# A graph layer's edge stage rebuilt: keys compared as products of sign codes, and a scatter with split sources and fp32 weights

## The reference, cut to what matters

```python
bias = jnp.full((n, n), NEG); bias = bias.at[diag, diag].set(0.0)
bias = bias.at[dst, src].set(edge_weight)      # of equal (dst, src) the last edge stays
scores = einsum('hnd,hmd->hnm', q, k) / 8 + bias[None]        # layer 0, 8 heads
sums = segment_sum(beta[dst], src)                            # layer 1: how often each edge occurs
adj = zeros((N, N)).at[edge_index[0], edge_index[1]].set(1.0) # layer 2: whether it occurs
```

## Time and profile before

| | us |
|---|---|
| median of 3 runs | 592.97 (591.87 to 593.33) |
| the profiled execution's own time | 593.2 |
| its span | 591.3 |
| PE busy | 482.4 |
| DVE busy | 357.6 |
| ACT busy | 205.7 |
| POOL busy | 149.2 |

### The profile page before, as it was taken

The page is one execution under the profiler, slowest core; times in us unless marked ns, Lnnn a source line. Parts: engine busy times, 40 slices in busy tenths (PEclk is TensorE's granted clock), DMA queues, the critical chain, the costliest instruction groups (busy, mean ns, idle before and its releaser), DMA issues.

```text
span 591.3 us, 9566 instructions
## 1 busy us (share of the span) xinstructions
PE 482.4 (82%) x3050; PEld 286.8 (48%) x3050; DVE 357.6 (60%) x890; ACT 205.7 (35%) x408; POOL 149.2 (25%) x153
## 2 busy tenths in 40 slices
PE   4999465677675699999799899767768679999996
PEld 2444222677665599944344444445533234444442
DVE  6699998788887996457813410369992520064305
ACT  1244233998986757322210111313332111101110
POOL 6033330333332810012100610055554110011000
PEclk9999865756766869999899999989988859999998
DMA  6994000000000300439240020000000000000001
GB/s 190 395 414 174 0 1 0 3 0 0 0 0 24 119 1 2 172 114 355 71 125 1 0 72 0 0 0 1 1 0 1 0 0 1 1 0 1 0 1 71
DMA packets 14456, 34.14 MB, mean 58 GB/s; under 512 B 992, under 2 KB 1504, under 8 KB 13920
## 3 DMA queue, kind: packets, MB, share of 16 engines
q1 hardware_dynamic: 14432, 33.83, 15.8%
HBM read 32.71 MB, written 1.11 MB: 57 GB/s over the span
## 4 chain that ended last, share of the span: by engine, by line
PE 48%; DVE 26%; issue 11%; ACT 5%; DVEq 4%; DMA 3%; POOL 2%; ACTq 1%; POOLq 0%; SPq 0%
PE ring L1002 33%; PE bank L1105 5%; PE ring L1008 4%; DVE RB L743 4%; DVE G L951 3%; DVE G L947 3%; DVE G L962 3%; DVEq L743 2%; PE ring L1201 2%; DMA G<-key_scratch 2%; DVE st L889 2%; ACT RB L552 2%; PE ring L1188 1%; DVE G L847 1%; DVE W_SD L797 1%
## 5 line engine op out<-in xcount | busy, mean ns | idle before, releaser
L1063 PE MATMUL bank<-rhs_now,X 128*128 128x64 bf16 x512 | 58.3, 210 | 23.5 <-DVE rhs_now L782 22.3
L743 DVE SCALAR_TENSOR_TENSOR RB<-G,tr,HH 128x256 bf16<-128x256 f32 (+1 forms) x128 | 64.3, 566 | 9.0 <-DMA G<-key_scratch 5.1
L1063 PEld LDWEIGHTS bank<-rhs_now,X 128*128 128x128 bf16 x512 | 50.6, 102 | 29.7 <-DVE rhs_now L782 29.4
L1064 PE MATMUL bank<-rhs_now,X 128*128 128x32 bf16 x512 | 57.3, 204 | 0.0
L1065 PE MATMUL bank<-rhs_now,X 128*128 128x32 bf16 x512 | 56.3, 185 | 0.0
L458 POOL TENSOR_TENSOR RB<-X,vec 128x512 f32<-128x512 f32 x16 | 21.9, 1379 | 125.0 <-DVE X L898 117.6
L1065 PEld LDWEIGHTS bank<-rhs_now,X 128*128 128x128 bf16 x512 | 52.7, 121 | 0.0
L1064 PEld LDWEIGHTS bank<-rhs_now,X 128*128 128x128 bf16 x512 | 51.0, 103 | 0.0
L438 POOL TENSOR_TENSOR A_SD<-A_SD,HH 128x128 f32 x64 | 30.6, 478 | 74.6 <-ACT HH L578 63.9
L909 DVE TENSOR_TENSOR HH<-ring,RB 128x512 f32<-128x512 f32 x16 | 11.0, 686 | 61.3 <-PE ring L1002 46.3
L1049 PE MATMUL ring<-KB,QB 64*128 64x512 f32 x64 | 29.5, 747 | 20.2 <-ACT G L519 20.2
(11 more groups left out here) (159 smaller groups left out, 965.2 us busy)
## 6 DMA issues: line engine op xcount, KB each, us to landing
G<-key_scratch SPq DMA_DIRECT2D x3, 2048.0 KB, 21.8
WAF<-in_wqkv SPq DMA_DIRECT2D x2, 1024.0 KB, 9.6
WB<-in_wo SPq DMA_DIRECT2D x2, 1024.0 KB, 17.0
WC<-in_w SPq DMA_DIRECT2D x2, 1024.0 KB, 17.0
WAF<-in_w SPq DMA_DIRECT2D x2, 1024.0 KB, 8.8
G<-in_w SPq DMA_DIRECT2D x1, 2048.0 KB, 14.7
G<-key_scratch SPq DMA_DIRECT2D x1, 1536.0 KB, 10.2
WAF<-in_xT SPq DMA_DIRECT2D x4, 256.0 KB, 5.4
```

The source lines that it names most:

```text
L743: dve.scalar_tensor_tensor(out=junk[:, j, 0:width], in0=G[:, bass.ds((t0 + j) * P, width)], scalar=keyT[:, bass.ds(t0 + j, 1)], in1=later_ ...
L1063: nc.tensor.matmul(gb[:, b, :, :], src1, rhs_now[:, q, j, 0:2, :], start=(j == 0), stop=False)
L1064: nc.tensor.matmul(gb[:, b, 1, :], src1, rhs_now[:, q, j, 2, :], start=False, stop=False)
```

## The change

**Keys.** The key becomes an integer of 18 bits. DVE takes each bit out (18 instructions), and one instruction makes it +16 or -16 in bf16. With three more rows (one, minus the position, the position, and constants) each tile has 24 rows of 128. SP stores these 768 KB and loads them back as `rows_l` and `rows_r`, with each code row on one partition, tiles 0 to 63 on partitions 0 to 20 and the rest from 64 on. A product of 21 rows is then above zero exactly where two keys are equal and the second position is later. TensorE makes three 128x128 products of each pair of tiles, and DVE takes the maximum of each row. Two such pairs make one step, of which there are 32, laid between the 16 products of K.

**Scatter.** The source is split into its low 7 bits, one-hot over 128 partitions, and its high 2 bits, which together with the dst in the window choose one of 128 columns. So a group is four 128x128 products: two bf16 for the counts and two fp32 for the weights. DVE makes the one-hots for four groups (eight tiles, a chunk, 16 in all) with one instruction each for sources and columns, and one for the fp32 weights; ACT widens the sources to fp32. `S` and `V` move into the scatter, two or three products ahead of each chunk.

**Clearing of the bias.** ACT writes `free` = relu(1 - count) beside the counts, and GpSimd multiplies the bias window by it, then adds the counts; DVE only adds the weights.

**Moved.** `wo0` is loaded after `bias_built`, since its tensor holds the wide sources. GpSimd adds the bias to V after its last group. `pe.wait_ge(tile_ranges, 2)`, ahead of Q, comes after the new codes on DVE.

```diff
             # SP
-            sp.dma_start(key_dram, nat[:, 3, :]).then_inc(key_stored, 16)
-                load(f"key{c}", G[:, part], flat[part].partition_broadcast(P))
+            sp.wait_ge(code_ready, 3)
+            sp.dma_start(code_dram, code).then_inc(code_stored, 16)
+            load("wk0", WA[:, 1, :, :], blocks(a["wqkv0"][:, D:2 * D]))
+            sp.wait_ge(code_stored, 16)
+            for i in range(2):
+                of_half = code_dram[i * (NT // 2):(i + 1) * (NT // 2), :, :]
+                part = slice(i * 64, i * 64 + ROWS)                      # ROWS = 21
+                sp.dma_start(by_tile(rows_l[part, :]), of_half[:, 0:ROWS, :].rearrange("t k e -> k t e")
+                             ).then_inc(loads["rows"], 16)
...                                     # rows_r: 18 rows, then 3 rows
             # GpSimd, for each group
+                held = W_SD[:, :, bass.ds(base, WIN)]
+                pool.wait_ge(free_ready, g + 1)
+                pool.wait_ge(group_folded, g + GI)
+                pool.tensor_tensor(held, held, free_g[:, q, :, :], ALU.mult).then_inc(bias_cleared, 1)
             # ACT
+            def widen(slot_, count, lap):
+                act.wait_ge(src_hot_ready, count)
+                if lap is not None:
+                    act.wait_ge(group_full, lap)
+                act.activation(src_wide[:, slot_, :, :, :], src_hot[:, slot_, :, :, :],
+                               ACT.Copy).then_inc(src_wide_ready, 1)
...
+                act.wait_ge(bias_cleared, g + 1)
+                act.activation(free_g[:, q, :, :], group_bank[q][:, 0, :, :], ACT.Relu, bias=one[:, :],
+                               scale=-1.0).then_inc(free_ready, 1)
+                act.activation(cnt_g[:, q, :, :], group_bank[q][:, 0, :, :], ACT.Copy).then_inc(count_ready, 1)
             # DVE
+            for k in range(CODE):                                       # CODE = 18
+                dve.tensor_scalar(bits_i[:, k, :], key_i, k, 1, ALU.logical_shift_right,
+                                  ALU.bitwise_and).then_inc(edges_float, 1)
...
+            dve.tensor_scalar(code[:, 3:ROWS, :], bits_i[:, :, :], 2.0 * BIT, -BIT, ALU.mult,
+                              ALU.add).then_inc(code_ready, 1)
...
+            def hot(out_, keys):
+                return dve.tensor_tensor(out_, iota_2[:, :, :].rearrange("p (q n) j -> p q n j", q=1).broadcast_to(
+                    [P, GI, P, 2]), keys.rearrange("p (q n j) -> p q n j", n=1, j=2).broadcast_to([P, GI, P, 2]),
+                    ALU.is_equal)                                       # all bf16
...
+            for p in range(PAIRS):                                      # PAIRS = 32
+                dve.wait_ge(pair_full, p + 1)
+                dve.tensor_reduce(later[:, 2 * p:2 * p + 2, :],
+                                  bank_all[:, p % 2 * 2:p % 2 * 2 + 2, 0:3 * P].rearrange("p r (c e) -> p r c e", e=P),
+                                  AX.X, ALU.max).then_inc(pair_taken, 1)
...
+                for c in range(NI):                                     # NI = 16
+                    word = dve.value_load(packed_i[0:1, c:c + 1], min_val=0, max_val=(1 << 28) - 1)
+                    g, more = c * GI, c + 2 < NI
+                    for q in range(GI):
+                        if more and q == GI - 2:
+                            dve.wait_ge(group_full, g + GI)
+                            dve.wait_ge(src_wide_ready, c + 1)
+                            src_hots(c % 2, chunk(lo_key, c + 2))
+                        if more and q == GI - 1:
+                            weight_hots(c % 2, chunk(last_weight, c + 2), c + 3)
+                        fold(g + q, q, window_start(word, q))
+                        if more and q == GI - 2:
+                            dst_hots(c % 2, chunk(column_key, c + 2))
             # TensorE
+            def compare(p):
+                if p >= 2:
+                    pe.wait_ge(pair_taken, p - 1)
+                for i in range(2):
...
+                    nc.tensor.matmul(to[:, 0:2 * P], rows_l[part, e:e + P], rows_r[part, e:e + 2 * P], start=True,
+                                     stop=True)
+                    last = nc.tensor.matmul(to[:, 2 * P:3 * P], rows_l[part, e + P:e + 2 * P],
+                                            rows_r[part, e + P:e + 2 * P], start=True, stop=True)
+                last.then_inc(pair_full, 1)
...
+                for j in range(2):
+                    nc.tensor.matmul(counts, src_hot[:, slot_, q, :, j], dst_hot[:, slot_, q, :, j], start=(j == 0),
+                                     stop=(j == 1), skip_group_check=True)
+                for j in range(2):
+                    last = nc.tensor.matmul(weights, src_wide[:, slot_, q, :, j], weight_hot[:, slot_, q, :, j],
+                                            start=False, stop=(j == 1), skip_group_check=True)
```

More of the change, by code:

```diff
@@ L34, with beside_scatter @@
 UNIT_HEADS = [0, 2, 1, 3, 4, 6, 5, 7]
+def beside_scatter():
+    return [[("S", 2 * (c // NB), c % NB), ("S", 2 * (c // NB) + 1, c % NB)] + ([("V", c // NB)] if c % NB == 1 else [])
+            for c in range(NI)]
 def ring_order():
@@ L49, in ring_order @@
         add("KT", (b,), "A")
[L50 to L54, removed]
+    for names in beside_scatter():
+        for name in names:
+            add(name[0], name[1:], "A")
     for b in range(NB):
@@ L192, in gnn_program @@
         tr = sb("tr", [P, 4, NT + 2 * GI])
[L193 to L209, removed]
+        loT, dstT, ewT, hiT = (tr[:, k, 0:NT] for k in range(4))
@@ L341, in _ @@
             load("x", X[:, :, :], blocks(a["x"]))
+            load("wo0", WB[:, :, :], blocks(a["wo0"]))
             wait_full(sp, ("BD", NB - 1))
@@ L455, in _ @@
             pool.engine_nop().then_inc(count_built, 1)
+            pool.wait_ge(loads["bv0"], 16)
+            for b in range(NB):
+                wait_emptied(pool, ("V", b))
+                pool.tensor_tensor(VB[:, b, :], VB[:, b, :], vec[:, slot["bv0"], :], ALU.add).then_inc(values_ready, 1)
             def resid(out_, x_, vector):
@@ new lines, in _ @@
+                for c in range(2):
+                    src_hots(c, chunk(lo_key, c))
+                    dst_hots(c, chunk(column_key, c))
+                for c in range(2):
+                    weight_hots(c, chunk(last_weight, c), c + 1)
+                for c in range(NI):
+                    word = dve.value_load(packed_i[0:1, c:c + 1], min_val=0, max_val=(1 << 28) - 1)
[10 more added lines that the diff above has]
+                            dst_hots(c % 2, chunk(column_key, c + 2))
@@ L1052, in group @@
[L1052 to L1066 removed]
+            pe.wait_ge(loads["rows"], 96)
@@ new lines, in _ @@
+            for b in range(NB):
+                t = claim(("KT", b))
+                for k in range(NB):
+                    last = nc.tensor.matmul(t[:, :], cols(WA[:, 1, :, :], k, b), XT[:, k, :], start=(k == 0),
+                                            stop=(k == NB - 1))
+                    if k == NB - 1:
+                        last.then_inc(ring_full, 1)
+                    for p in range(2):
+                        compare((b * NB + k) * 2 + p)
+            wait_emptied(pe, ("KT", NB - 1))
@@ new lines, in _, with beside @@
+            pe.wait_ge(loads["wv0"], 16)
+            def beside(c):
+                for name in beside_scatter()[c]:
+                    if name[0] == "V":
+                        product(name, lambda k: cols(XT, k, name[1]), lambda k: WA[:, 2, k, :])
+                    else:
+                        h, b = name[1:]
+                        r = slice((h % 2) * HD, (h % 2 + 1) * HD)
+                        nc.tensor.matmul(claim(name)[:, :], QB[r, h // 2, b * P:(b + 1) * P], KB[r, h // 2, :],
+                                         start=True, stop=True).then_inc(ring_full, 1)
@@ new lines, in hots, with group @@
+            def hots(count):
+                pe.wait_ge(src_hot_ready, count)
+                pe.wait_ge(dst_hot_ready, count)
+                pe.wait_ge(src_wide_ready, count)
+                pe.wait_ge(weight_hot_ready, count)
+            def group(g, q, slot_):
+                pe.wait_ge(group_folded, g + 1)
+                counts, weights = bank[q][:, 0:P], bank[q][:, P:2 * P]
+                for j in range(2):
[4 more added lines that the diff above has]
+                                            start=False, stop=(j == 1), skip_group_check=True)
```

378 lines of the change are left out of this document (165 added, 213 removed).

## The result

The changed kernel took 608.70 us (607.58 to 612.85, 4 runs) against 592.42 us (590.54 to 593.33, 4 runs) for the kernel before beside it: ratio 1.0275, 95% interval 1.0243 to 1.0306. It is slower, outside the range of 561 to 603 us, and the forecast of 579 us was wrong in sign and size. The span of its profiled execution is 606.5 us.

The account below looks back on a forecast made before the run. The prediction saw DVE's comparisons as the bound up to 99.5 us, then no single engine but a loop of ACT and DVE taking turns. It summed 593.2 - 15.3 + 1 = 579 us, range 561 to 603.

Parts of the forecast that it names:

- Step 1: Codes on DVE and their store: codes ready at 14.3 us, store 4.3 us, done at 18.6.
- Step 2: Loading the code rows back: rows land at 40 us (bounds 30 and 75).
- Step 3: Comparing: 32 steps set by DVE's maxima take 33 us (31 to 36), ending at 73.
- rival D: Comparing and chunks with V: PE becomes the bound in places at the low clock, 8+3 us more, 590; chance 0.12.
- Step 4: From comparing into the scatter, through flags, branch register and first one-hots: first add to W at 81 us.
- Step 5: The scatter's pace: 1.06 us a group, 6.06 a chunk, 93.3 us in all, `bias_built` at 174 against 189.4.
- Step 6: Behind the scatter: GpSimd's adds to V hold DVE's first row minima, 1 us late.
- B: Scatter: the relay between GpSimd and DVE is slow, scatter 111 or 127 us, total 597 to 612; chance 0.14.
- A: Loading rows back: pieces sit on few engines, rows at 60 us or later, 20 us more, 599; chance 0.12.
- C: Row loads and scatter: packets spread evenly (rows at 31), relay of 0.9 us, 19 less, 560; chance 0.15.

Follow-up runs that it names:

- fill: The changed kernel with eight unused products of 128 rows and 512 columns in PE's wait for the rows: 586.38 us, 0.9914 of the kernel before.
- w_bf16: fill with the weights and their source one-hots in bf16 instead of fp32: 588.77 us, 0.9910 of the kernel before.

## Why the prediction was wrong, step by step

- **Step 1** right: the store was issued at 14.16 and took 4.11 us (14.3 and 4.3 forecast).
- **Step 2** right: first product at 39.38 (40), with a 6.76 us wait ahead. I wrote that "nothing covers this" and priced the wait at its own length. I didn't ask what it does to PE's clock afterwards.
- **Step 3 failed.** The term was "two steps have one of these", a product at 0.43 or 0.90 us. The earlier trace rows says x32 and x8, and I took these for products; they are instructions, two to a product. With 0.90 the low clock gave 1.12 us a step, "late by 0.1 us", and so rival D priced it at 3 us. With 2.0 it is 1.70, and the stage took 55.5 us instead of 33: 22.5 of the 30 us by which the bias turn missed. Neither error would have done it alone: fill has the right count at full clock, and its stage takes 32.5 us (39.85 to 72.4); the low clock with my count takes 36.
- **Step 4**: 8.6 us from the end of comparing to the first fold, against 8 (the terms that I wrote down add up to 7.2). The branch register took 1.10 us; the 0.90 that I cited is a wait for ACT, as the earlier trace rows says. One-hots of 0.68 us where undisturbed, as taken.
- **Step 5** missed by 7.5 us (100.8 against 93.3). A group is 1.28 and not 1.06: into GpSimd it took 0.17 and not 0.24, but from the end of GpSimd's multiply to DVE's fold 0.36, where I took 0.07 from an edge that ACT releases. The Trainium skill (Perfetto Trace Analysis, section GPSIMD Engine Instruction) advises to time GpSimd's instructions from start to start and not by their spans. The trace agrees that the span isn't the price of a hand-over: from the start of the multiply to the start of the add that it releases are 0.82 us, against a span of 0.46. The one-hots cost 1.1 a chunk and not 1.82, so by luck the errors nearly cancel in a chunk (6.24 against 6.06, 2.5 us in all). The fifteenth chunk is 0.9 longer, the first chunk with V, at the end of the low clock, 2.4, the other three 0.4 each, the third chunk 0.4. The halved price of step 3 stands here too: I gave PE 3.9 us at full clock for a chunk with V (1.3+0.9+1.7). In the trace it is 7.2, more than a chunk's 6.24: 1.06 for S (105.36 to 106.42), 3.54 for V (to 109.96) and 0.64 for each of four groups.
- **Step 6**: 0.4 us instead of 1.
- **Rivals.** D had the mechanism (PE the bound in places because it stays at the low clock) and half its size. B, the side on which it ended, priced the relay nearly right (1.34 a group) but isn't what made the kernel slower: with the relay's 1.28, fill is faster than before. A's and C's landings didn't come. The split of the chances isn't what its own rule gives: 0.755 faster and 0.195 slower, not 0.73 and 0.22.

The sum with the measured terms: 579 + 22.5 + 0.6 + 7.5 - 0.6 for the rows - 0.6 behind = 608.4 us, the changed kernel's time.

Why it isn't faster than before: DVE's first add to `W_SD` stood at 104.79 in the kernel before and comes at 103.51, so the stages ahead of it gained 1.3 us; from there to the bias turn it took 84.7 us before and takes 100.8. With the clock held (fill) the first part is 23.8 us better and the second 16.2 worse, 7.7 us less in all. The second part is longer because its chunks are: 5.1 to 5.6 us each before, but for the first, and 6.24 now.

## What to carry to other kernels

Divide the count of matmul instructions in a row by the products in the code before pricing one. When a change puts a wait of several microseconds ahead of work on TensorE, price that work at the low clock too, count all that shares the engine there, and look whether something can fill the wait. Price a hand-over from GpSimd by starts in a trace of the same pair of engines.

## What the runs showed of the hardware

- In the six traces in which PE waited 3.4 to 7.6 us for the rows its clock fell to 0.50, within the wait or in the first 2 us behind it. In the changed kernel it stayed there while the engine was busy for 55.14 of 55.60 us, and came back to 1.00 only in the scatter (0.50 up to 105 us, 0.93 from 105 to 106, 1.00 behind). With the same work and no wait it stood at 1.00 for 30 us (fill). I had expected a busy engine to get its clock back.
- Less work for PE needn't gain anything: with 13 us less of it in the scatter the granted clock went from 0.92 to 0.76, and w_bf16 was no faster than fill (588.77 against 586.38 us).
- Fourteen percent more pieces landed 3.4 to 4.2 us earlier, as 24 partitions instead of 21, than in four traces with 21; a fifth with 21 landed 0.5 to 0.7 us behind them.
